# First pass of a Mamba-and-two-FFN block: a row's turn moved into the next step, and Dskip applied where the y product is evacuated

## What is computed

```python
x = x + 0.5 * ffn(layernorm(x))          # ternary weight, 1024x1024, + bias
xn = layernorm(x)
u, z = split(xn @ W_in.T)                # 1024 channels each
u = silu(conv_b + sum(conv_w[:, k] * shifted(u, k) for k in range(4)))
x_dbl = u @ W_xproj.T                    # 64 columns for dt, 16 for B, 16 for C
dt = softplus(x_dbl[..., :64] @ W_dt.T + b_dt)
y = scan(exp(dt * A), dt * B * u, C)     # state of 16 per channel, over 4096 tokens
y = (y + u * Dskip) * silu(z)
x = x + y @ W_out.T
x = x + 0.5 * ffn(layernorm(x))
```

## Time and profile before

| | us |
|---|---|
| median of 3 runs | 3046.5 (3045.56 to 3048.08) |
| the profiled execution | 3049.45 |
| its span | 3047.7 |
| mean granted TensorE clock | 0.905 of full speed |
| busy over the span: TensorE, VectorE, ScalarE, GpSimd | 2480.6, 2552.9, 1922.3, 1963.9 |

### The profile page before, as it was taken

The page is one execution under the profiler, slowest core; times in us unless marked ns, Lnnn a source line. Parts: engine busy times, 40 slices in busy tenths (PEclk is TensorE's granted clock), DMA queues, the critical chain, the costliest instruction groups (busy, mean ns, idle before and its releaser), DMA issues.

```text
span 3047.7 us, 42676 instructions
## 1 busy us (share of the span) xinstructions
PE 2480.6 (81%) x12448; PEld 1412.7 (46%) x12448; DVE 2552.9 (84%) x3357; ACT 1922.3 (63%) x3432; POOL 1963.9 (64%) x1577
## 2 busy tenths in 40 slices
PE   3578889888888736788888888888888889898887
PEld 1233444344343314555555555555555545555553
DVE  5566766766766559999999999999999999999992
ACT  2234756756765666666766767667666766666663
POOL 1112222222221138899999989989989989999993
PEclk8688999999999857798999999999999998989999
DMA  5554323323322262221221221222222222212101
GB/s 195 179 193 146 111 103 120 104 105 125 104 98 105 84 218 104 73 76 52 91 80 46 90 79 55 78 81 65 77 74 73 74 73 75 74 60 90 59 28 42
DMA packets 159779, 286.76 MB, mean 94 GB/s; under 512 B 40928, under 2 KB 90336, under 8 KB 157216
## 3 DMA queue, kind: packets, MB, share of 16 engines
q1 hardware_dynamic: 159520, 283.71, 27.8%
HBM read 174.09 MB, written 109.58 MB: 93 GB/s over the span
## 4 chain that ended last, share of the span: by engine, by line
POOL 30%; issue 14%; DVE 13%; PE 5%; ACT 1%; POOLq 1%; DMA 0%; DVEq 0%; SPq 0%; ACTq 0%
POOL dbu L1042 23%; DVE h L1265 8%; DVE y L1277 4%; PE p_g L1387 3%; POOL y L1059 2%; PE p_ht L1353 1%; POOL o L1084 1%; POOL carry L1053 1%; POOL x L1078 1%; POOL dbu L1047 1%; POOLq L41 1%; PE p_g L1377 0%; DVE q L1290 0%; POOL y L1074 0%; POOL small L70 0%
## 5 line engine op out<-in xcount | busy, mean ns | idle before, releaser
L1265 DVE TENSOR_TENSOR_SCAN h<-p_da,dbu 128x512 f32<-128x512 f32 x1024 | 1190.9, 1203 | 50.8 <-ACT p_da L1147 32.9
L1147 ACT ACTIVATE p_da<-dt_,neg_a 128x255 f32<-128x255 f32 x2048 | 885.4, 467 | 511.1 <-DVE h L1265 509.3
L1042 POOL TENSOR_TENSOR dbu<-dtu,bb 128x1024 f32<-128x1024 f32 x512 | 1198.2, 2363 | 0.6
L1353 PE MATMUL p_ht<-ident,h 128*128 128x128 f32 x4096 | 604.2, 307 | 185.8 <-DVE h L1265 184.2
L1353 PEld LDWEIGHTS p_ht<-ident,h 128*128 128x128 f32 x4096 | 534.0, 159 | 288.1 <-issue 143.1
L1277 DVE SCALAR_TENSOR_TENSOR y<-p_ht,ct,y 128x1024 f32<-128x1024 f32 x432 | 544.9, 1261 | 5.2 <-PE p_ht L1353 5.1
L359 POOL TENSOR_TENSOR late<-dt,u 128x512 f32<-128x512 f32 x64 | 82.4, 1288 | 426.0 <-DVE dt L552 426.0
L1387 PE MATMUL p_g<-wo,tokt 128*128 128x512 f16 x1536 | 353.6, 388 | 1.6 <-ACT tokt L1179 1.6
L710 PE MATMUL p_u<-xz,wu 128*128 128x512 f16 x1536 | 351.1, 386 | 0.0
L1396 PE MATMUL p_g<-wz,xz 128*128 128x512 f16 x1536 | 350.9, 386 | 0.0
L70 POOL TENSOR_TENSOR small<-small,consts 128x1 f32<-128x1 f32 x96 | 60.8, 633 | 409.8 <-DVE small L63 409.7
(11 more groups left out here) (120 smaller groups left out, 3011.4 us busy)
## 6 DMA issues: line engine op xcount, KB each, us to landing
bb<-b_scratch SPq DMA_DIRECT2D x128, 256.0 KB, 3.3
xin<-in_x SPq DMA_DIRECT2D x32, 512.0 KB, 4.3
x_scratch<-x SPq DMA_DIRECT2D x32, 512.0 KB, 3.3
xz_scratch<-xz SPq DMA_DIRECT2D x16, 1024.0 KB, 6.5
y_scratch<-late SPq DMA_DIRECT2D x32, 512.0 KB, 2.9
dt_scratch<-dt SPq DMA_DIRECT2D x64, 256.0 KB, 2.2
dtu_scratch<-late SPq DMA_DIRECT2D x64, 256.0 KB, 2.5
dt_<-dt_scratch SPq DMA_DIRECT2D x64, 256.0 KB, 3.5
```

The costliest lines, as they stand in the source:

```text
L1042: nc.gpsimd.tensor_tensor(state[:, 4 * f:4 * f + 4, :], dtu[par][:, 4 * f:4 * f + 4, :], bb[n // NB % 2][:, n % NB:n % NB + 1, :].to_broad ...
L1147: ins_ = nc.scalar.activation(p_da[p % 2][:, k * T2 + 1:(k + 1) * T2], dt[:, g, 1:], ACT.Exp, scale=neg_a[:, g, n:n + 1])
L1265: nc.vector.tensor_tensor_scan(h[n % 2][:, 2 * p:2 * p + 2, :].rearrange("p g t -> p (g t)"), p_da[p % 2][:], dbu[n % 2][:, 2 * p:2 * p + ...
L1353: mm = nc.tensor.transpose(p_ht[t][:, g * P:(g + 1) * P], h[n % 2][:, g, t * P:(t + 1) * P], ident[:])
```

## The change

The first pass alone is changed. The order in each engine's step is rewritten, the units are reordered, and Dskip moves.

- A step now begins with `turn(1, k-1)` of the row before (`turned` says when there is one), with its `high` and `low`; `ffn(k)` follows. `turn(0, k+1)`, `high(0, k+1)` and `low(0, k+1)` stand in the second half of step k. The semaphores of the two kinds of turn are separate.
- VectorE adds the FFN product and takes its statistics ahead of all s phases; phase 0 follows, then the convolution of 2j, `low(0, k+1)`, and phases 1 to 3.
- GpSimd's s phases all come last in its step.
- The store of xz moves to the next step 0, behind the stores of phases 0 and 1. The row load keeps its place.
- `dskip` is loaded as a row broadcast to 128 partitions (512 KB); TensorE transposes u itself, and VectorE multiplies by dskip as it empties the bank. `ud` is gone.

```diff
-        units = [("y", 0), ("y", 1), ("x", 0), ("c", 0), ("d", 0), ("y", 2), ("d", 1), ("d", 2), ("y", 3), ("d", 3),
-                 ("y", 4), ("d", 4), ("y", 5), ("d", 5), ("d", 6), ("y", 6), ("d", 7), ("y", 7)]
+        units = [("y", 0), ("x", 0), ("y", 1), ("c", 0), ("d", 0), ("y", 2), ("d", 1), ("y", 3), ("d", 2), ("d", 3),
+                 ("y", 4), ("d", 4), ("y", 5), ("d", 5), ("y", 6), ("d", 6), ("d", 7), ("y", 7)]
         per_phase = [(1, 1, 1, 1), (1, 1, 1, 2), (1, 1, 1, 1), (1, 2, 1, 1)]
...
+                         (dskip[:], ins["Dskip"].partition_broadcast(P))]
...
 # SyncE, step, after the stores of phases 0 and 1 and the weight loads
+                    if j == 0 and turned(k, f_on):
+                        for b in range(2):
+                            wait_alone(sp, tr_split[1][b], k)
...
+                                         xz[par][:, a].rearrange("p h k t -> p h (k t)")).then_inc(xz_stored[par], 16)
 # ScalarE, step
+                    if turned(k, f_on):
...
+                            high(1, k - 1, into[:, 0, jj // 2, 4 * b:4 * b + 4, (jj % 2) * P:(jj % 2 + 1) * P], b)
+                    if had_u(i, j):
+                        u_work(*before)
+                    if f_on and not last(k):
+                        normalise(0, xin[(j + 1) % 2][:], k + 1)
+                    if s_on:
+                        s_work(i - 1, j, 0)
+                    if had_u(i, j):
+                        silu(before[0], par if j else 1 - par, before[1])
+                    w_high(i, j, slice(0, 2))
+                    if f_on:
+                        normalise(1, x1[j % 2][:], k)
+                    if s_on:
+                        s_work(i - 1, j, 1)
+                    if u_on:
+                        u_work(i, 2 * j)
+                    if f_on and not last(k):
+                        wait(act, ffn_full, k * 2 + 2)
+                        for b in range(2):
+                            high(0, k + 1, xt[:, 0, 4 * b:4 * b + 4, :], b)
                     w_high(i, j, slice(2, None))
+                    if s_on:
                         s_work(i - 1, j, 2)
+                    if u_on:
+                        silu(i, par, 2 * j)
                     if s_on:
                         s_work(i - 1, j, 3)
 # VectorE, step: low(1, k-1); row_stats of k+1; conv(before); then x1 and its row_stats as before
+                    w_work(i, j, slice(0, 2))
                     if s_on:
+                        s_work(d, 1 - par, j, 0)
+                    if u_on:
+                        conv(i, 2 * j)
+                    if f_on and not last(k):
+                        for b in range(2):
+                            low(0, k + 1, xt[:, 0, 4 * b:4 * b + 4, :], xt[:, 1, 4 * b:4 * b + 4, :], b)
+                    w_work(i, j, slice(2, None))
                     if s_on:
+                        s_work(d, 1 - par, j, 1)
+                        s_work(d, 1 - par, j, 2)
                         s_work(d, 1 - par, j, 3)
 # VectorE, a y unit
-                            nc.vector.tensor_copy(y0[g // 2 % 2][:, :, (g % 2) * P:(g % 2 + 1) * P],
...
+                            nc.vector.tensor_tensor(y0[g // 2 % 2][:, :, (g % 2) * P:(g % 2 + 1) * P],
+                                                    p_s[v % 2][:].rearrange("p (t n) -> p t n", t=TT1),
+                                                    dskip[:, g * P:(g + 1) * P].unsqueeze(1).to_broadcast([P, TT1, P]),
+                                                    ALU.mult).then_inc(s_free[v % 2], 1)
 # TensorE, step
+                    if turned(k, f_on):
+                        turn(1, k - 1)
                     if f_on:
                         ffn(k)
                     if s_on:
+                        s_work(i - 1, 1 - par, j, 0)
                     if u_on:
...
                         u_product(i, par, 2 * j)
                     if s_on:
+                        s_work(i - 1, 1 - par, j, 1)
+                    if f_on and not last(k):
+                        turn(0, k + 1)
                     if u_on:
                         u_product(i, par, 2 * j + 1)
+                    if s_on:
+                        s_work(i - 1, 1 - par, j, 2)
+                        s_work(i - 1, 1 - par, j, 3)
```

More of the change, by code:

```diff
@@ L165, in first_pass @@
         s_free = [sem(f"s_free{i}") for i in range(2)]
-        ud_done, y0_stored = sem("ud_done"), [sem(f"y0_stored{i}") for i in range(2)]
+        y0_stored = [sem(f"y0_stored{i}") for i in range(2)]
         b_stored, ct_stored = sem("b_stored"), sem("ct_stored")
@@ L383, in step @@
                     if s_on:
-                        s_work(i - 1, 1 - par, j, 2)
-                        s_work(i - 1, 1 - par, j, 3)
+                        for phase in range(4):
+                            s_work(i - 1, 1 - par, j, phase)
                 drive(pool, step, prologue)
@@ L458, in step @@
                 def step(i, par, j, f_on, u_on, s_on):
-                    f = i + 1
-                    k = f * TT1 + j
+                    k = (i + 1) * TT1 + j
                     before = (i if j else i - 1, (2 * j - 1) % G)
[L462 to L483, removed]
+                    if turned(k, f_on):
+                        f, jj, into = (i + 1, j - 1, xz[1 - par]) if j else (i, TT1 - 1, xz[par])
+                        if jj == 0:
                             wait(act, u_full, (f - 1) * G)
@@ L552, in s_work @@
                             nc.vector.tensor_tensor(dt[g % 2][:], res[:], rel[g % 2], ALU.add).then_inc(dt_done, 1)
-                def times_dskip(d, dpar, g):
-                    b, m = unit_at(d, "y", g - 2) if g >= 2 else unit_at(d - 1, "y", g + 6)
-                    wait(dve, s_full[b], m)
-                    wait(dve, silu_done, d * G + g + 1)
-                    nc.vector.tensor_scalar(ud[g % 2][:], u[dpar][:, g, :], dskip[:, g:g + 1], None,
-                                            ALU.mult).then_inc(ud_done, 1)
                 steps = [0]
@@ L597, in prologue @@
                     dve.wait_ge(const_loaded, 16 * 7)
+                    for b in range(2):
+                        low(0, 0, xt[:, 0, 4 * b:4 * b + 4, :], xt[:, 1, 4 * b:4 * b + 4, :], b)
                 def factor(m):
@@ L637, in step @@
                     k = f * TT1 + j
[L638 removed]
+                    if turned(k, f_on):
+                        jj, into = (j - 1, xz[1 - par]) if j else (TT1 - 1, xz[par])
                         for b in range(2):
[L640 to L645 removed]
+                            hi, lo = (into[:, a, jj // 2, 4 * b:4 * b + 4, (jj % 2) * P:(jj % 2 + 1) * P] for a in range(2))
+                            low(1, k - 1, hi, lo, b)
+                    if f_on and not last(k):
+                        wait(dve, x_loaded[(j + 1) % 2], (f * 2 + (j + 1) // 2 + 1) * 16)
+                        row_stats(dve, nc, xin[(j + 1) % 2], stats[0], mv[0], vn[0], small[:, 40:41], ln_chain[0],
+                                  stats_ready[0], scale_ready[0], k + 1)
                     if had_u(i, j):
                         conv(i if j else i - 1, (2 * j - 1) % G)
[L648 to L650 removed]
                     if f_on:
@@ L685, in turn @@
                     for b in range(2):
-                        wait(pe, tr_split[b], k * 2 + n)
+                        if n:
+                            if not last(k):
+                                wait(pe, tr_split[0][b], k + 2)
+                        else:
+                            wait(pe, tr_split[1][b], k - 1)
                         for q in range(4):
@@ L765, in step @@
                         u_product(i, par, 2 * j)
-                    if f_on:
-                        turn(1, k)
                     if s_on:
-                        s_work(i - 1, 1 - par, j, 3)
+                        s_work(i - 1, 1 - par, j, 1)
+                    if f_on and not last(k):
+                        turn(0, k + 1)
                     if u_on:
                         u_product(i, par, 2 * j + 1)
+                    if s_on:
+                        s_work(i - 1, 1 - par, j, 2)
+                        s_work(i - 1, 1 - par, j, 3)
                 drive(pe, step, prologue)
```

96 lines of the change are left out of this document (34 added, 62 removed).

## The result

The changed kernel takes 3077.9 us (median of 4 runs, 3074.6 to 3079.0) against 3046.0 (3043.9 to 3048.1): slower, ratio 1.0104 with a 95% interval of 1.0089 to 1.0119. The forecast was 3065, the range 3005 to 3085. The profiled execution took 3077.43 us for 3049.45, with a span of 3075.6 for 3047.7 and a mean granted clock of 0.903 for 0.905.

A forecast was written before the change was run, and what follows sets the result against it. ScalarE's and VectorE's fixed-order queues were taken to bound the kernel. 15.0 + 4.5 - 5.1 + 0.6 + 1.2 + 2.4 = +18.6 on 3049.45 gave 3068.0, less 2.95 to the median 3065; range 3005 to 3085, likeliest 3053 to 3077.

The forecast's parts named there:

- The bound: First pass, middle blocks: ScalarE's and VectorE's fixed-order queues decide; ScalarE has 68.2 us against TensorE's 69.5 in steps 1 to 3.
- Steps 1 to 3: Middle block laid out by engine: ScalarE idle 3.8, 9.4 and 6.2 us; the block takes 119.1 us for 116.1.
- Five periods: Middle of the first pass, unit x at 273.87 to 854.17: 3.0 us more in each period, +15.0.
- Next and last interval: End of the first pass: last block with an FFN 114.9 us, +4.5; the one without FFN 84.5, -5.1.
- Up to the first x: Start to the first unit x: dskip's load +1.2, the turn in block -1 at 0, block 0 +2.4.
- the turn in block -1: Block -1: the moved turn is hidden by VectorE's wait for the row's DMA, 0 (bounds -2.5 and +1).
- the third weight part: Block 0: it stands behind the convolution of 2j, delaying the next row load, +2.4 (bounds 0 and +12.7).
- Dropping `ud`: VectorE: eight instructions of 0.48 us fewer a block, none on the path, so 0 (bounds 0 and -3.8 a block).
- The multiplication: VectorE's y evacuation: 0.6 us like the copy it replaces; at 1.5 it would cost 1.8 a block, +9.
- A: Step 3: the row is in time, statistics start 3.4 us earlier, block 115.7, time 3048, no change; 10 in 100.
- B: Pipelining works, no bank or row wait ends late: block 99.7, 2968 us, 9 in 100; half, 3017, 15.
- C: More lost: dear y evacuations (+9), block 0's +12.7, or lower clock through FFN rows (+6.5): 3072 to 3091; 9 in 100.

The follow-up runs named there:

- e2: Changed kernel with VectorE's s phase 1 moved ahead of the convolution of 2j and low(0, k+1): 3031.8 us, ratio 0.9949.
- e1: Changed kernel with SyncE's x1 store and row load issued ahead of the stores of phases 0 and 1: 3061.6 us, ratio 1.0049.
- e5: Kernel before with the Dskip part alone (broadcast load, u transposed, multiplication at the evacuation, no ud): 3037.5 us, ratio 0.9972.
- e9: e8 with VectorE, in blocks 1 and later, doing low(0, k+1) right behind phase 1's y evacuation, its d unit behind the convolution: 2982.9 us, ratio 0.9795.
- e6: Changed kernel with the xz store issued behind the x1 store and row load of step 0: 3067.1 us, ratio 1.0079.
- e8: Changed kernel with phase 1, row load, ScalarE's copy and high early, xz store late, block 0's low and weight part ahead of the convolution: 3011.4 us.
- e4: Changed kernel with the multiplication by dskip left out, the y unit copied plainly from its bank: 3075.0 us, ratio 1.0092.

## Why the prediction was right, and where its sizes were off

**The bound.** It said that ScalarE's and VectorE's fixed queues decide, not TensorE's work, and that turning rows in another step wins nothing by itself. TensorE's busy time in the block is 101.2 for 101.9, and moving a call or two on VectorE took the block from 119.4 to 113.1 and from 111.6 to 107.8. Right. The size was not: 3077.9 lies within the range of 3005 to 3085 but just outside the likeliest case's own, 3053 to 3077, and the loss of 31.8 is well above the 18.6 of the sum.

**Steps 1 to 3.** Laid out from the start of step 1 (773.93 in the trace), step 2 was to start at 24.6 and step 3 at 55.5, d7 at 88.15 and the next block's step 1 at 119.1. Measured: 24.9, 54.8, 87.6 and 119.4. ScalarE's idle 3.8, 9.4 and 6.2 came as 3.64, 9.22 and 6.37, TensorE's waits as 6.10 and 9.90. Each of the two causes was then taken away alone: y's place on VectorE (e2) and the load's place in SyncE's queue (e1). What the path of this block left out is the clock behind the wait before d7: the turn after it took 1.91 and step 0's FFN row 8.06, together 1.9 us over their length in step 1. Most of it is given back on the way: from d7 to the next block's step 1 it is 31.8 us for the 31.0 laid out.

**Five periods, +15.0 forecast, +20.6 measured.** Four of the five are 3.0 to 4.5 over those of before, as the trace has them, 14.1 together for 12.0. The remaining one, the third, is 6.6 over: it holds two waits that the profile puts down to "issue", 4.30 on VectorE at 633.78 and 1.02 on TensorE at 623.59. Each stands before its engine's first instruction of the step with which the loop over pairs of blocks begins its second turn. The kernel before has no such wait and no longer period (116.05 there); e5, which has its order, has both (2.41 on VectorE, 115.9 for 112.7), and e9 has the waits (2.92 and 3.37) with a period only 0.6 longer. No run takes the waits away, so their cause stays open.

**Next and last interval.** +4.5 came as +4.15. -5.1 came as -2.7: the method is a few us off where ScalarE's units follow each other with nothing else between, and I did not follow that up.

**Up to the first x, +3.6 forecast, +4.85 measured,** and here the agreement is luck: three errors nearly cancel. Split it at the row that block -1 loads last, whose statistics begin at 145.94 before and 143.52 after.
- Up to that row: -2.4, where I had +1.2 for dskip's load and 0 for the turn in block -1 (bounds -2.5 and +1). ScalarE's wait for dskip does end 1.38 later, but in e5, which has this load and the old order, the row comes at 145.99: the load costs nothing by then. The new order is worth some 2.4 there, the edge of my bounds; which move gives it was not tried.
- The xz store: +3.9 (e6), where I had nothing. This is the missed term. The prediction names the store as standing ahead of a row load in the middle blocks, where there is slack, and never asks the same of block 0, where VectorE waits for that row.
- The rest of block 0, the third weight part among it: 7.3 less 3.9 leaves +3.4 (135.2 us for 127.9 from that row to the first x), where I had +2.4. With the weight part and `low` ahead of the convolution e8 wins some 6 us, so the convolution's shade was not free.

**Dropping `ud` at 0.** e5 shows it worth 3.4 us a block in the order of before, through one wait in step 0. That it is worth nothing in the new order I only argued: none of its instructions stands on the path laid out, and that path came out right, but no run has the new order with `ud`.

**The multiplication at 0.6 a unit.** 0.68 busy, and e4 gains nothing clear of noise; the rival's 1.5 us never appeared. The prediction worked out from the Trainium skill (GPSIMD Engine Reference, section 1, Specifications) that an instruction with one input in PSUM would not be held up by GpSimd. The trace agrees: all 64 of them take 678 to 693 ns, where line 559 of the kernel before went from 474 to 1497.

**The rivals.** A (the row in time, 3048) was the right mechanism with the right price: e1 makes its condition true and the block falls by 3.1 for 3.4. It had only 1 chance in 10, and rightly, since SyncE's order had not been written for it. B (the pipelining works) needs several more moves than the change has; with those of e9 the block is 107.8, not the 99.7 that B named, and the time 2983, not 2968. C's size of 3072 to 3091 (9 in 100) holds the result, but its two large causes did not come: neither the dear multiplication nor 12.7 for the weight part. Its third came in part: the lower clock held into step 0's FFN row, 1.0 us of the 1.3 a block. The rest is a store in a queue and one longer period.

The sum was mis-sized, +18.6 for +27.9, in these terms: the xz store in block 0 (3.9) and the longer period (3.6 above forecast) are missing, the other four periods are 2.1 too low together, the rest of block 0 is 1.0 too low, the part up to block -1's last row 3.6 too high, and the last interval gave 2.4 less than I took.

## What to carry to other kernels

Work that is pipelined by moving it to another place in a hand-written queue moves everything behind it too: for every call that you move, write down what each engine does until the next bank or buffer comes free, the engine that only issues DMAs included, and do so in the first blocks as well as in the steady ones. A small evacuation on which the main engine waits belongs ahead of long chains, and a longer piece should not be moved forward in the same bundle with it: splitting the y copy from the d unit beside it, and putting one `low` ahead of the convolution, was worth 28 us. The place of a late transfer can cost 23 us or 2, depending on what else is late. And before a shift at one point of a single trace is put down to an edit, look whether the trace was already ahead where the edit cannot act yet: here 5 of 9 us were.

## What the runs showed of the hardware

After an idle stretch TensorE runs at the lower of its two clock levels for a while: behind 6.10 us of waiting eight transposes took 1.91 us for 1.04, and behind 9.90 us a d unit 2.07 for 1.12, and the turn after it still 1.91; the granted clock of each of these three stretches was 0.50. A wait of 1.75 us (e9, at 764.58) hardly slowed the turn behind it (1.16, clock 0.98), but the clock was 0.50 over the first 2 us of the FFN row after that, which took 8.73 for 7.07. The block's mean granted clock was 0.91 with 18.2 us of waits, 0.96 with 14.2 in the kernel before, and 0.97 with 7.5 in e9. I had put nothing of this on the path but d7's one.

A 512 KB row load was there 4.6 us after its issue in the middle block shown (833.74 to 838.30). The one in block 0's first step took 13.3 us behind 2 MB of xz and a weight load in SyncE's queue, and 12.4 to 14.4 in the five other traces with that order; with the xz store issued behind it, it took 10.1 to 10.7 in four traces.
